# A two-layer network with a residual: the last pair of products of the last tile in two halves of its columns, the last row stored in three pieces

## The reference

```python
h = jax.nn.gelu(jnp.einsum('bnd,hd->bnh', x, fc1_w) + fc1_b, approximate=False)
shared = jnp.einsum('bnh,sh->bns', h, fc2_w) + fc2_b
We = experts_w[indices]
be = experts_b[indices]
expert_x = jnp.einsum('bnh,bph->bnp', h, We) + be[:, None, :]
return x + jnp.concatenate([shared, expert_x], axis=-1)
```

## Time and profile before

| what | us |
|---|---|
| median of 3 runs | 357.48 (357.47 to 357.76) |
| profiled execution, in all | 357.54 |
| its span, first to last instruction | 355.4 |
| TensorE busy (2381 matmuls) | 350.9 |
| VectorE busy | 259.5 |
| ScalarE busy | 246.8 |
| GpSimd busy | 235.0 |
| DMA, mean over the span | 106 GB/s |

### The profile page before, as it was taken

The page is one execution under the profiler, slowest core; times in us unless marked ns, Lnnn a source line. Parts: engine busy times, 40 slices in busy tenths (PEclk is TensorE's granted clock), DMA queues, the critical chain, the costliest instruction groups (busy, mean ns, idle before and its releaser), DMA issues.

```text
span 355.4 us, 7075 instructions
## 1 busy us (share of the span) xinstructions
PE 350.9 (99%) x2381; PEld 323.7 (91%) x2381; DVE 259.5 (73%) x498; ACT 246.8 (69%) x410; POOL 235.0 (66%) x150
## 2 busy tenths in 40 slices
PE   8999999999999999999999999999999999999996
PEld 5899899999999999999999999999999999999996
DVE  2797976968859697786968869697786968844642
ACT  4885957777678577767777678577777777666560
POOL 0179887658866586865758866576865758855471
PEclk9999999999999999999999999999999999999999
DMA  8779663533333334341533324353332230312001
GB/s 239 172 162 191 140 181 85 148 99 89 112 87 117 89 90 141 94 110 59 149 98 89 114 79 122 90 137 101 84 107 64 90 99 30 120 38 89 31 30 61
DMA packets 69981, 37.53 MB, mean 106 GB/s; under 512 B 43450, under 2 KB 69946, under 8 KB 69946
## 3 DMA queue, kind: packets, MB, share of 16 engines
q1 hardware_dynamic: 69376, 36.55, 38.1%
q10 hardware_dynamic: 570, 0.53, 0.4%
HBM read 28.68 MB, written 8.39 MB: 104 GB/s over the span
## 4 chain that ended last, share of the span: by engine, by line
PE 98%; ACT 0%; issue 0%; POOL 0%; DVE 0%; POOLq 0%; ACTq 0%
PE fc_ps L1110 40%; PE acc_ps L1166 29%; PE acc_ps L1169 15%; PE fc_ps L1086 6%; PE acc_ps L1136 3%; PE acc_ps L1189 2%; PE fc_ps L1166 1%; PE fc_ps L1052 1%; PE fc_ps L1093 1%; PE fc_ps L1169 1%; PE tr_ps L1046 0%; ACT xt L461 0%; PE tr_ps L1068 0%; ACT w1t L474 0%; DVE resid L906 0%
## 5 line engine op out<-in xcount | busy, mean ns | idle before, releaser
L395 POOL TENSOR_TENSOR ht<-gelu,ht 128x1024 fp32r<-128x1024 f32 x62 | 149.5, 2411 | 97.4 <-ACT ht L565 97.4
L1166 PE MATMUL acc_ps<-w2t,ht 128*128 128x512 f32 x448 | 162.4, 397 | 0.0
L1110 PE MATMUL fc_ps<-xt,w1t 128*128 128x256 f32 x1176 | 159.9, 284 | 0.0
L1110 PEld LDWEIGHTS fc_ps<-xt,w1t 128*128 128x128 f32 x1176 | 148.7, 189 | 5.5
L1169 PE MATMUL acc_ps<-w2t,ht 128*128 128x256 f32 x448 | 125.9, 281 | 0.0
L1166 PEld LDWEIGHTS acc_ps<-w2t,ht 128*128 128x128 f32 x448 | 84.4, 188 | 14.9
L1169 PEld LDWEIGHTS acc_ps<-w2t,ht 128*128 128x128 f32 x448 | 85.0, 190 | 0.0
L565 ACT ACTIVATE ht<-gelu 128x1024 fp32r<-128x1024 f32 x64 | 68.0, 1063 | 3.6 <-issue 0.4
L591 ACT ACTIVATE gelu<-work,b 128x512 f32<-128x512 f32 x56 | 37.3, 715 | 26.2 <-DVE work L870 26.1
L403 POOL TENSOR_TENSOR xt<-work,xt 128x1024 fp32r<-128x1024 f32 x14 | 33.8, 2417 | 14.8 <-ACT xt L554 14.8
L870 DVE TENSOR_TENSOR work<-fc_ps,work 128x512 f32<-128x512 f32 x28 | 19.4, 692 | 22.6 <-PE fc_ps L1110 21.3
(11 more groups left out here) (73 smaller groups left out, 335.6 us busy)
## 6 DMA issues: line engine op xcount, KB each, us to landing
pieces<-in_L_cond_experts_w SPq DMA_DIRECT2D x128, 64.0 KB, 2.0
out<-resid SPq DMA_DIRECT2D x31, 256.0 KB, 3.1
pieces<-in_x SPq DMA_DIRECT2D x60, 128.0 KB, 2.9
resid<-in_x SPq DMA_DIRECT2D x15, 512.0 KB, 3.5
e_bias<-in_L_cond_experts_b SPq DMA_DIRECT2D x32, 32.0 KB, 2.8
work<-in_L_cond_fc_w SPq DMA_DIRECT2D x4, 256.0 KB, 4.7
w_piece<-in_L_cond_fc_w SPq DMA_DIRECT2D x4, 192.0 KB, 5.0
resid<-in_x SPq DMA_DIRECT2D x2, 256.0 KB, 3.2
```

The source lines that it names most:

```text
L395: nc.gpsimd.tensor_tensor(ht[:, slot, LO, :, :].rearrange("p k t -> p (k t)"), gelu[:, q % GELUS, :, :].rearrange("p k t -> p (k t)"), ht[ ...
L1110: last = nc.tensor.matmul(fc1_ps[:, dst, j * SEQ:(j + 1) * SEQ], w1t[:, w, wv, ms], xt[:, n % 2, o, xv, :], start=(fresh and j == 0 and at ...
L1166: nc.tensor.matmul(acc.rearrange("p (v o) -> p v o", v=2), ht[:, q % SLOTS, HI, j, ts], w2t[:, :, k, fc2_columns(b)], start=(k == 0), stop ...
```

## The change

The pair r = 3 of tile 1 of the last row, until now six matmuls of 256 columns, becomes two calls of `fc2_last` with six matmuls each of 128 columns. The first call adds columns 0 to 127 to `acc_ps[:, 1]`, where pairs 0 to 2 already are. The second puts columns 128 to 255 into `fc1_ps` bank 0, starting afresh there, after a wait for `c21_gelu`. VectorE adds `acc_ps[:, 1]` with all its 256 columns once the first half is done (now told by `tile_filled`), and then `fc1_ps` bank 0 to the upper 128 columns once the second half is done (`fc2_done`). The last row is stored by three DMAs: tile 0 with 128 KB, and the two halves of tile 1 with 64 KB each, 512 bytes for each token. SyncE waits for one landing more.

```diff
@@ drained_at
-            per_tile = 1 if n == LAST and b == 1 else 2 * additions(b)
+            if n == LAST and b == 1:
+                return 3 + 12 * (n - 1) + 8 * b + 2 * t + 1
+            per_tile = 2 * additions(b)
             return 3 + 12 * (n - 1) + 8 * b + per_tile * (t + 1)
@@
         LAST = BLOCKS - 1
+        last_parts = [(t, slice(0, OUT)) for t in range(T - 1)]
+        last_parts += [(T - 1, slice(h * OUT // 2, (h + 1) * OUT // 2)) for h in range(2)]
@@ sync
-            for t in range(T):
-                sp.wait_ge(drained, drained_at(LAST, 1, t))
-                sp.dma_start(out_blocks[LAST][:, T + t, :], resid[:, LAST % 2, T + t, :])\
+            for t, cols in last_parts:
+                sp.wait_ge(drained, drained_at(LAST, 1, t) - (cols.start == 0 and t == T - 1))
+                sp.dma_start(out_blocks[LAST][:, T + t, cols], resid[:, LAST % 2, T + t, cols])\
                     .then_inc(stored[LAST % 2], 16)
             for par in range(2):
-                sp.wait_ge(stored[par], 16 * (R * (BLOCKS // 2) + (par == LAST % 2)))
+                sp.wait_ge(stored[par], 16 * (R * (BLOCKS // 2) + 2 * (par == LAST % 2)))
@@ vector, drain_last
                 for t in range(T):
-                    if t == 0:
-                        dve.wait_ge(tile_filled, tile_at(LAST, 1))
-                    else:
-                        dve.wait_ge(fc2_done, fc2_end(LAST, 1, PAIRS - 1))
+                    dve.wait_ge(tile_filled, tile_at(LAST, 1) + t)
                     dst = resid[:, LAST % 2, T + t, :]
                     nc.vector.tensor_tensor(dst, acc_ps[:, t, 0:OUT], dst, ALU.add)\
                         .then_inc(drained, 1)
+
+                dve.wait_ge(fc2_done, fc2_end(LAST, 1, PAIRS - 1))
+                dve.wait_ge(drained, drained_at(LAST, 1, T - 1) - 1)
+                dst = resid[:, LAST % 2, R * T - 1, OUT // 2:OUT]
+                nc.vector.tensor_tensor(dst, fc1_ps[:, 0, OUT // 2:OUT], dst, ALU.add)\
+                    .then_inc(drained, 1)
@@ tensor
-            def fc2_last(t, r):
+            def fc2_last(t, r, cols=slice(0, OUT)):
+                fresh = r == 0 or cols.start > 0
+                if cols.start > 0:
+                    pe.wait_ge(c21_gelu, 2 * LAST_T)
                 q = PAIRS * LAST + r
                 wait_h_lo(pe, q)
@@
                     for v, w in ((HI, HI), (HI, LO), (LO, HI)):
-                        last = nc.tensor.matmul(acc_ps[:, t, 0:OUT], ht[:, q % SLOTS, v, j, ts],
-                                                w2t[:, w, k, fc2_columns(1)],
-                                                start=(k == 0 and v == HI and w == HI), stop=True,
-                                                skip_group_check=True)
-                if t == T - 1 and r != 2:
+                        acc = fc1_ps[:, 0, cols] if cols.start > 0 else acc_ps[:, t, cols]
+                        last = nc.tensor.matmul(acc, ht[:, q % SLOTS, v, j, ts],
+                                                w2t[:, w, k, PART:PART + OUT][:, cols],
+                                                start=(fresh and j == 0 and v == HI and w == HI),
+                                                stop=True, skip_group_check=True)
+                if t == T - 1 and (r < 2 or r == PAIRS - 1 and cols.start > 0):
                     last.then_inc(fc2_done, 1)
@@
             for t in range(T):
-                for r in range(2, PAIRS):
-                    fc2_last(t, r)
+                fc2_last(t, 2)
+                for at, cols in last_parts:
+                    if at == t:
+                        fc2_last(t, PAIRS - 1, cols)
```

## The result

The changed kernel takes 358.16 us (median of 22 runs, 357.81 to 358.65), the kernel before 357.61 us (median of 22, 357.28 to 358.57). The ratio is 1.0014, with a 95% interval of 1.0008 to 1.002: 0.5 us slower (0.3 to 0.7), which is inside the 0.2% that were set as the bound of no change. The forecast started from the median of the first three runs of the kernel before, 357.48; over all 22 it is 357.61. The profiled execution took 358.10 us, with a span of 355.9 us against 355.4.

A forecast was written before the change was run, and what follows sets the result against it. TensorE, busy 99% of the span, was taken to bound the kernel. +0.72 for TensorE, -0.135 for the add and -0.11 for packets gave +0.48 us on 357.48: 357.9 us forecast, range 357.2 to 359.3.

The forecast's parts named there:

- likeliest case: Whole kernel: narrow matmuls 0.12 us apart and fewer packet costs in the last store, 357.7 to 358.2 us, chance 0.50.
- TensorE, mis-sized: Last pair of the last tile: twelve 128-column matmuls for six of 256 columns run 0.72 us longer.
- The distance of 0.12: Start-to-start spacing in us claimed for the twelve 128-column matmuls at the end, the same as for 256 columns.
- the transposes: Eight L1068 transposes, 128 four-byte columns with 128x128 weight loads, start 0.12 us apart; taken as the nearest row.
- the row of the exposed weight load: 512-column matmuls at 348.11 and 349.28: 0.51 us with load held back, 0.40 with it hidden; load about 0.11 us.
- The waits cost nothing: Two further waits on TensorE, h_lo and c21_gelu, already fulfilled before the last matmuls: nothing, 0.08 us at most.
- VectorE: End of kernel: 256-column add hidden under the second six matmuls; last 128-column add takes 0.285 us, saving 0.135 us.
- The last store, mis-sized: Final store of 64 KB in 512-byte packets, 31 ns for 45 each: saves 0.11 us, bounds nothing to 0.18.
- narrow matmuls cost half: Last twelve matmuls 0.06 us apart, TensorE ends as before: 357.34 to 357.37 us; chance 0.12 for 0.06 to 0.09.
- they cost what 512 columns do: Last twelve matmuls run in several passes, 0.23 us apart: +1.8 us, 359.3 us, chance 0.20.
- the landing does not come sooner with fewer bytes: Last store: its 1.73 us hardly depend on bytes, so halving saves nothing: +0.59 us, 358.1 us, chance 0.14.

The follow-up runs named there:

- the single store: Changed kernel with the last tile stored by one DMA of 128 KB behind both adds: 358.21 us, ratio 1.0019.
- the second set: The kernel before and the changed kernel run again, each with only an empty line added: 357.49 us and 358.14 us.

## Why the prediction was right, and where it was not

The forecast was no change, at 357.9 us (+0.48 us in its sum), and +0.5 us (0.3 to 0.7) came: 358.16, at the upper end of the likeliest case (357.7 to 358.2), with the kernel before at 357.61 and not 357.48. The direction of every term held; the sum agrees better than its terms.

- **TensorE, mis-sized.** The step that narrow matmuls are hardly closer together than wide ones, since each waits for its weights, was right. The distance of 0.12 was not: it is 0.111 to 0.112 us, and 0.06 once, at the first narrow pair. The prediction had called itself wrong if the distance is not 0.12; by that sign its mechanism stands, and its size is 7% too high. The term was +0.57 us and not +0.72. I had taken the distance from the transposes; the row of the exposed weight load, 0.11 us, stood beside it and was the nearer one. By the Trainium skill's "TensorE: Matmul & The Clock Gate", section "LDWEIGHTS (loading the stationary operand)", a load of 128 columns takes 107 ns, and this case's 0.111 agrees with it to 4%. The sustained 81 ns that the same page of the Trainium skill gives for 128 columns in its section "Back-to-back issue gap" is not met by these matmuls of four-byte data, which stay 0.111 us apart; its 56 ns for an isolated gap is near the single distance of 0.06.
- **The waits cost nothing.** Right for the wait for `c21_gelu`: 357.48 us with it, 357.51 without. In the trace after, the matmul behind both waits starts 0.11 us after the one ahead of it, like the others.
- **VectorE.** Right: the add of 256 columns is hidden, the add of 128 took 0.292 us for my 0.285, and saved 0.13.
- **The last store, mis-sized.** 0.18 us saved, for my 0.11 and at the end of my bounds. A packet of 512 bytes takes 28 ns and not 31, one of 1024 takes 48 and not 45: both means that I used were mixtures.
- **What no step had:** 0.15 to 0.25 us outside of the span. The runs show that it goes with VectorE's list and not with the wait on TensorE; its cause is open. I had taken the 2.1 us around the span as given.

By the measured terms the sum is +0.57 - 0.13 - 0.18 + 0.2 = +0.46 us. Two terms were too high together by 0.22 and one was missing, of about that size, so 357.9 came close for a reason that was partly luck. In the second set the changed kernel's mean span was 0.43 us longer where the tail gives 0.26. The mean spans of the other variants stand 0.13 us below to 0.08 above what their tails give, so a tenth of a microsecond either way is scatter of the start; the 0.17 us here are little more than that, and I can't give them a cause of their own.

The rivals: that narrow matmuls cost half, and that they cost what 512 columns do, both fell by the distance of 0.11. That the landing does not come sooner with fewer bytes fell by the single store, for 128 against 64 KB. From 64 to 32 KB it stays open.

## What to carry to other kernels

Splitting matmuls by columns to let the next engine begin sooner is paid in weight loads: as soon as a matmul streams for less time than its load takes, each piece costs a whole load (0.11 us here). Twelve pieces at 0.11 us in place of six at 0.12, less the short first distance, cost 0.57 us against the 0.31 us that a smaller add and a smaller store gave back. Before such a split, set the number of pieces times the exposed load from the trace, less what the wide matmuls took, against what the tail behind the last matmul can lose at all. Where effects are of a few tenths of a microsecond, compare the spans and what lies outside of them separately, and make controls that change an engine's list and nothing of its work, of more than one length.

## What the runs showed of the hardware

- Matmuls of four-byte data with a 128x128 weight load each start 0.11 us apart at 64, 128 and 192 columns, 0.12 at 256 and 0.23 at 512, at the full clock (granted 1.00). At 64 and 128 columns their weight loads start 0.112 us apart. The first distance of such a row, behind wider matmuls, is 0.05 us at 64 columns, 0.06 at 128 and 0.09 at 192. By 0.12 / 256 us for a column, streaming takes as long as the load at about 240 columns, an estimate.
- A store of 128 rows of 1024 bytes releases its waiter 1.73 us behind the issue, one of 128 rows of 512 bytes 1.55 us, one of 256 bytes, close behind a larger one, also 1.55 us. The second of two stores of 64 KB issued 0.2 to 0.4 us apart takes 1.61 to 1.64 us.
- The time of an execution outside of the recorded span is 2.08 to 2.18 us with 692, 693 and 698 records in VectorE's list and 2.30 to 2.37 us with 694, in four programs, each a mean.
- Fulfilled waits that stand as instructions of their own ahead of an add delay it by 0.1 us: it starts 0.13 to 0.14 us behind the end of its matmul and not 0.04, in two runs.
